# Experts' results weighted at the banks and scattered to the rows of the tokens' choices

## What is computed

```python
def _L1_ffn_ref(hidden_states, gate_w, gate_up_proj, down_proj):
    x = hidden_states.reshape(-1, H)
    probs = jax.nn.softmax(x @ gate_w.T, axis=-1)
    w, idx = jax.lax.top_k(probs, TOP_K)
    w = w / jnp.sum(w, axis=-1, keepdims=True)
    combine = jnp.zeros((T, E), x.dtype).at[jnp.arange(T)[:, None], idx].add(w)
    def step(acc, inputs):
        gup, dn, ce = inputs
        g, u = jnp.split(x @ gup.T, 2, axis=-1)
        acc = acc + ce[:, None] * (jax.nn.silu(g) * u @ dn.T)
        return (acc, None)
    ...
x = x + jnp.tanh(g_ffn[1]) * _L1_ffn_ref(_layernorm(x, axis=-1), ...)
```

## Time and profile before

| | us |
|---|---|
| median of 3 runs (lowest to highest) | 677.53 (677.33 to 678.94) |
| the profiled execution, its own time | 676.72 |
| its span, first to last instruction | 675.0 |
| PE busy in the span | 591.9 (88%) |
| DVE busy | 396.9 (59%) |
| POOL busy | 324.8 (48%) |
| ACT busy | 292.7 (43%) |

### The profile page before, as it was taken

One profiled execution on the slowest core, in us unless ns is written; L12 is line 12 of the kernel. 1 busy time (PEld: TensorE's weight loads), 2 busy tenths in 40 slices (PEclk: granted clock), 3 DMA queues, 4 the chain that ended last, 5 costly groups with the idle time before them and its releaser, 6 DMA issues.

```text
span 675.0 us, 12862 instructions
## 1 busy us (share of the span) xinstructions
PE 591.9 (88%) x5214; PEld 454.9 (67%) x5214; DVE 396.9 (59%) x790; ACT 292.7 (43%) x565; POOL 324.8 (48%) x248
## 2 busy tenths in 40 slices
PE   4699999999889999999999999975299999989920
PEld 3466666667656667676766767554299999889910
DVE  6465557666755455575555656585256666556524
ACT  2144444454433544454444445552066665266300
POOL 4957457755700255453644545594143343234135
PEclk9799999999999999999999999966599999999975
DMA  8900695000000000000000000350421855351024
GB/s 264 303 2 1 252 416 208 2 2 1 3 2 1 1 1 1 1 15 1 15 1 14 15 1 15 147 241 7 163 101 51 349 205 199 121 203 40 26 62 122
DMA packets 22487, 60.33 MB, mean 89 GB/s; under 512 B 3041, under 2 KB 12945, under 8 KB 19089
## 3 DMA queue, kind: packets, MB, share of 16 engines
q1 hardware_dynamic: 19792, 54.82, 21.7%
q0 software_dynamic: 1536, 3.67, 1.8%
q10 hardware_dynamic: 1088, 0.88, 0.5%
HBM read 39.70 MB, written 19.66 MB: 88 GB/s over the span
## 4 chain that ended last, share of the span: by engine, by line
PE 69%; POOL 15%; DVE 8%; issue 3%; ACT 2%; DMA 2%; POOLq 0%; DVEq 0%; ACTq 0%
POOL sr L1442 10%; PE ps L54 8%; PE ps L55 7%; PE ps L56 7%; PE ps L545 6%; PE ps L574 6%; PE ps L622 4%; PE ps L604 4%; PE ps L591 4%; DVE KN L893 3%; PE ps L471 2%; PE ps L654 2%; PE ps L561 2%; PE ps L490 2%; PE ps L430 2%
## 5 line engine op out<-in xcount | busy, mean ns | idle before, releaser
L1473 POOL TENSOR_SCALAR P<-P,rinv 112x487 f32<-112x487 f32 x64 | 97.9, 1540 | 97.6 <-DVE rinv L926 97.6
L1153 POOL TENSOR_TENSOR WL<-WR,WH 128x1024 fp32r<-128x1024 f32 x24 | 60.5, 2519 | 97.2 <-ACT WH L1400 97.2
L1442 POOL TENSOR_TENSOR sr<-sv,mhalf 125x32 f32<-125x32 f32 x16 | 87.0, 5438 | 1.3
L54 PE MATMUL ps<-XGf,WH 128*128 128x256 f32 x256 | 74.0, 289 | 2.1 <-DVE XGf L1088 1.4
L55 PE MATMUL ps<-XGf,WH 128*128 128x256 f32 x256 | 73.6, 288 | 0.0
L56 PE MATMUL ps<-XGf,WL 128*128 128x256 f32 x256 | 73.6, 288 | 0.0
L893 DVE TENSOR_REDUCE KN<-ps 112x4 f32<-112x1500 f32 x32 | 55.0, 1720 | 27.4 <-PE ps L471 27.3
L1279 ACT ACTIVATE P<-ps,nm 112x487 f32<-112x487 f32 x64 | 42.1, 662 | 60.9 <-DVE nm L918 60.9
L1230 ACT ACTIVATE P<-ps 125x1344 f32<-125x1344 f32 x32 | 41.3, 1292 | 43.6 <-PE ps L490 43.6
L918 DVE TENSOR_REDUCE nm<-ps 112x1 f32<-112x487 f32 x64 | 39.5, 659 | 30.4 <-PE ps L591 30.4
L1153 DVE TENSOR_TENSOR WL<-WR,WH 128x1024 fp32r<-128x1024 f32 x24 | 46.9, 1956 | 10.5 <-ACT WH L1400 10.4
(11 more groups left out here) (194 smaller groups left out, 1319.2 us busy)
## 6 DMA issues: line engine op xcount, KB each, us to landing
WR<-in_gupT SPq DMA_DIRECT2D x16, 1024.0 KB, 6.8
WR<-in_dwnT SPq DMA_DIRECT2D x8, 1024.0 KB, 10.5
xs<-ZT SPq DMA_DIRECT2D x14, 512.0 KB, 5.8
ys<-ZT SPq DMA_DIRECT2D x14, 512.0 KB, 6.1
P<-xs SPq DMA_DIRECT2D x24, 128.0 KB, 5.9
CT<-in_ctxT SPq DMA_DIRECT2D x1, 2250.0 KB, 10.4
ys<-WS SPq DMA_DIRECT2D x16, 128.0 KB, 1.8
Wk<-in_L_xattn_Wk SPq DMA_DIRECT2D x2, 512.0 KB, 10.6
```

The costliest lines, as they stand in the source:

```text
L54: e.matmul(out, ah, bh, start=start, stop=False)
L1153: e.tensor_tensor(WL[x % 3][:, cs], WR[x % 3][:, cs], f_(WH[x % 2][:, cs]), ALU.subtract).then_inc(split_done(x, c)[0], 1)
L1442: e.tensor_tensor(sr[:, p, :], sv[:, p, :], mhalf[0:125, 0:32], ALU.pow).then_inc(s("sr"), 1)
L1473: e.tensor_scalar(P[:, k, 0:487], P[:, k, 0:487], rinv[:, k:k + 1], None, ALU.mult).then_inc(s("psc"), 1)
```

## The change

Each row of xs grows from 256 to 258 values (`ROW`): a token's row carries its weight for this choice, tanh of the gate included, and the number of its row in the new ys. For that a second copy of the normalized tokens is kept (`XN2`, copied by ACT, `_2` in the trace), so that the two choices have different tails. ys now has 896 rows for first choices, 896 for second choices, and rows of their own for the empty places of the experts' tiles; it is no longer filled with zeros.

In the experts' loop each load of 128 rows of xs becomes two DMAs, of 256 values into XG and of the last 2 into the tile EX. The copies out of the result banks multiply by the weight in EX. DVE works out the 3 x 128 rows of ys of an expert (`rows_of`, two small operations). SP's stores of results become scatters on POOL, three per expert, the third (`oversent`) also where `over` did not run. At the end SP loads both choices' rows of a sequence with one plain DMA each (8 of 224 KB), and DVE adds the two to X.

```diff
@@ expert_order
             if pdc == 3:
+                put("sent", p)
                 put("over", p)
+                put("oversent", p)
@@ DVE: weights of a token's two choices
-                e.tensor_tensor(q["w1"], q["v1"], q["s2"], ALU.mult).then_inc(s("rchain"), 1)
-                e.tensor_tensor(q["w2"], q["v2"], q["s2"], ALU.mult).then_inc(s("rchain"), 1)
+                for to, v in ((XN, "v1"), (XN2, "v2")):
+                    e.scalar_tensor_tensor(to[:, b, D:D + 1], q[v], q["s2"], tg[0:NQ, 3:4], ALU.mult,
+                                           ALU.mult).then_inc(s("rchain"), 1)
@@ ACT, xtc
+                    if r == 3:
+                        w.wait_ge(s("rconst"), 9)
+                        e.activation(XN2[:, b, 0:D], XN[:, b, 0:D], ACT.Copy).then_inc(s("xn2"), 1)
@@ DVE, hid
-                    n = 4 * i[0] + i[1]
+                    x, n = i[0], 4 * i[0] + i[1]
+                    if i[1] == 1:
+                        for k in (2 * (x % 2), 2 * (x % 2) + 1):
+                            w.wait_ge(s(f"xg{k}"), 32 * (x // 2 + 1))
+                        w.wait_ge(s("xg4"), 32 * (x + 1))
+                        rows_of(e, w, x, slice(0, 3), 2 * x)
...
+        def rows_of(e, w, x, t, at):
+            given = EX[:, x, t, 1].bitcast(I32)
+            w.wait_ge(s("rconst"), 11)
+            e.scalar_tensor_tensor(rows_f[:, x, t], given, 0.0, own[:, x, t], ALU.is_equal,
+                                   ALU.mult).then_inc(s("rows"), 1)
+            w.wait_ge(s("rows"), at + 1)
+            e.tensor_tensor(rows_i[:, x, t], rows_f[:, x, t], given, ALU.add).then_inc(s("rows"), 1)
@@ DVE and ACT, copies out of the banks
-                    e.tensor_copy(YS[:, k, :], ps[:, 5, 0:256]).then_inc(s("yc0"), 1)
+                    e.tensor_scalar(YS[:, k, :], ps[:, 5, 0:256], weight(x, 0), None, ALU.mult).then_inc(s("yc0"), 1)
...
-                    e.activation(YS[:, k, :], ps[:, 6, 0:256], ACT.Copy).then_inc(s("yc1"), 1)
+                    e.activation(YS[:, k, :], ps[:, 6, 0:256], ACT.Copy, scale=weight(x, 1)).then_inc(s("yc1"), 1)
@@ POOL, experts
+                elif stage == "sent":
+                    x, = i
+                    w.wait_ge(s("rows"), 2 * x + 2)
+                    for t_ in range(2):
+                        k = 2 * (x % 2) + t_
+                        w.wait_ge(s(f"yc{t_}"), x + 1)
+                        scatter(e, result_rows(x, t_), YS[:, k, :]).then_inc(s(f"y{k}"), 16)
+                elif stage == "oversent":
+                    x, = i
+                    w.wait_ge(s("tile_act"), 6 * (x + 1))
+                    scatter(e, result_rows(x, 2), YSo).then_inc(s("tile_y"), 16)
@@ POOL, combination
-                    e.indirect_dma_start(Y2[0:NQ, k, :], None, ys,
-                                         bass.IndirectOffsetOnAxis(ap=i_[:, b:b + 1], axis=0)).then_inc(s(f"g{k}"), 16)
@@ SP, experts
-                        e.dma_start(XG[:, k, :], xs[row:row + 128, :]).then_inc(s(f"xg{k}"), 16)
+                        e.dma_start(XG[:, k, :], xs[row:row + 128, 0:D]).then_inc(s(f"xg{k}"), 16)
+                        e.dma_start(EX[:, x, t_, :], xs[row:row + 128, D:ROW]).then_inc(s(f"xg{k}"), 16)
...
-                        e.dma_start(ys[row:row + 128, :], YS[:, k, :]).then_inc(s(f"y{k}"), 16)
@@ SP, combination
+            for k in range(4):
+                w.wait_ge(s(f"y{k}"), 16 * (NE // 2))
+            w.wait_ge(s("tile_y"), 16 * NE)
             for b in range(NB):
-                w.wait_ge(s("comb"), 3 * (b + 1))
+                src = ys[1:1 + 2 * NT, :].rearrange("(c t) d -> t c d", c=2)[b * NQ:(b + 1) * NQ]
+                e.dma_start(Y2[:, b, :, :], src).then_inc(s(f"in_y{b}"), 16)
+            for b in range(NB):
+                w.wait_ge(s("comb"), 2 * (b + 1))
                 e.dma_start(out[b, :, :], X[:, b, :]).then_inc(s("out"), 16)
@@ DVE, combination
+                w.wait_ge(s(f"in_y{b}"), 16)
+                for c in range(2):
+                    w.wait_ge(s("comb"), 2 * b + c)
+                    e.tensor_tensor(X[:, b, :], X[:, b, :], Y2[:, b, c, :], ALU.add).then_inc(s("comb"), 1)
```

More of the change, by code:

```diff
@@ L20 @@
 EPS = 1e-5
+ROW = D + 2
 class Order:
@@ L319, in build, with weight, result_rows, scatter @@
         tri, ones = sq[0:NQ, 0, 0:NQ], sq[0:NQ, 1, 0:NQ]
-        xs = nc.dram_tensor("xs", [NE * NT, D], F).ap()
-        ys = nc.dram_tensor("ys", [NE * NT, D], F).ap()
+        XN2 = B["_2"][0:NQ, 0:NB * ROW].rearrange("p (a b) -> p a b", a=NB)
+        EX = sb("EX", [128, NE, 3, 2])
+        own, own_i, rows_f, rows_i = (sb(n, [128, NE, 3], d) for n, d in
+                                      (("own", F), ("own_i", I32), ("rows_f", F), ("rows_i", I32)))
+        Y2 = B["WR2"][0:NQ, 0:NB * 512].rearrange("p (b c d) -> p b c d", b=NB, c=2)
+        xs = nc.dram_tensor("xs", [NE * NT, ROW], F).ap()
+        ys = nc.dram_tensor("ys", [2 * NT + NE * 3 * 128 + 1, D], F).ap()
+        def weight(x, t_):
+            return EX[:, x, t_, 0:1]
+        def result_rows(x, t_):
+            return bass.IndirectOffsetOnAxis(ap=rows_i[:, x, t_:t_ + 1], axis=0)
+        def scatter(e, rows, src):
+            return e.indirect_dma_start(ys, rows, src, None)
         PTf = PF[:, 1536:5120]
@@ L773, in pairs_out, with sent_before @@
                 w.wait_ge(s(f"pair{k}"), 1 + max(u // 3 for u in before if u % 3 == k))
+        def sent_before(w, x, k):
+            if k:
+                w.wait_ge(s(f"far_y{x}"), 16 * k)
+            else:
+                w.wait_ge(s("tile_y"), 16 * NE)
+                w.wait_ge(s("far_done"), x)
         def skipped(e, sem, before, by):
@@ L1392, in scalar_tile @@
             w.wait_ge(pe, 6 * k + 6)
-            e.activation(YSo, ps[:, 6, 0:256], ACT.Copy).then_inc(act, 1)
+            e.activation(YSo, ps[:, 6, 0:256], ACT.Copy, scale=weight(x, 2)).then_inc(act, 1)
         def split_high(e, w, x, c):
@@ L1467, in pool_attention @@
                                     pattern=[[1, NQ]], channel_multiplier=-1).then_inc(s("rconst"), 1)
+                    w.wait_ge(s("qt2"), NQUAD)
+                    w.wait_ge(s("spk"), order.total["spk"])
+                    w.wait_ge(s("spq"), NB)
+                    for k, to in enumerate((XN, XN2)):
+                        e.iota(to[:, :, D + 1:ROW].bitcast(I32), pattern=[[NQ, NB], [0, 1]], base=1 + k * NT,
+                               channel_multiplier=1).then_inc(s("rconst"), 1)
+                    e.iota(own_i[:, :, :], pattern=[[384, NE], [128, 3]], base=1 + 2 * NT,
+                           channel_multiplier=1).then_inc(s("rconst"), 1)
+                    w.wait_ge(s("rconst"), 10)
+                    e.tensor_copy(own[:, :, :], own_i[:, :, :]).then_inc(s("rconst"), 1)
                 elif stage == "sc":
@@ L1568, in sync_experts @@
                     if x >= 1:
[L1569 removed]
+                        w.wait_ge(s("xg4"), 32 * x)
+                        w.wait_ge(s("tile_pe"), 6 * (x - 1) + 1)
                     row = x * NT + 256
[L1571 to L1588 removed]
+                    e.dma_start(XG[:, 4, :], xs[row:row + 128, 0:D]).then_inc(s("xg4"), 16)
+                    e.dma_start(EX[:, x, 2, :], xs[row:row + 128, D:ROW]).then_inc(s("xg4"), 16)
+                elif stage == "over" and i[0] == 0:
+                    count = counts(e, w)
                 elif stage == "far":
@@ L1640, in _ @@
             pool_experts(e, w)
-            pool_combine(e, w)
         @block.scalar
```

136 lines of the change are left out of this document (57 added, 79 removed).

## The result

The changed kernel took 693.42 us (median of 4 runs, 690.37 to 696.47), beside 677.43 us for the kernel before (4 runs, 676.96 to 678.94): a ratio of 1.0232, 95% interval 1.0183 to 1.0281. The forecast of 668.7 us and its range missed it, on the side of "slower".

The account below looks back on a forecast made before the run. PE bounds the kernel (69% of the chain of waits), except after the last matmul, where it idles 29.80 us. -12.0 + 0.2 + 3.0 = -8.8 us on 676.72 gives 667.9, median 668.7 us; range 664.5 to 677.0.

Parts of the forecast that it names:

- the order on the resource that DVE and POOL share: Among the experts: `hid`, c1, c2, c3 take turns, c3 ends late, PE waits 0.6 us in five experts, +3.0 us.
- the second rival: Among the experts: POOL's c1 gets ahead of DVE's `hid`, 2.1 us for each of five experts; 676.2 us, chance 0.30.
- rows_of: Among the experts: its two small DVE operations cost 0.2 us each and move the following `hid` from 517.40 to 517.80.
- The slack: Among the experts: after PE's wait for c3 the rest follows within PE's slack of some 2 us.
- The scatters: Ahead of c1 in an expert: 1.05 us if awaited, 0.95 us else; 128 rows in proportion add 0.4 us.
- The third rival: Among the experts: scatters slow beside weight loads, deciding from 2.2 us each; at 2.5 us, 682.2 us; chance 0.11.
- Five experts: The wait happens in the first four experts and the sixth, 0.6 us each.
- PE waits for c2: Sign among the experts: PE waiting for c2 would show the prediction wrong.
- Routing to experts: Between routing and experts: DMAs doubled on SP delay PE's third transpose, +0.2 us, bounds 0 to 0.6.
- The end: Last copy to the end: scatters, eight loads and 16 DVE additions finish sooner, -12.0 us, bounds -13 to -10.
- Start and attention: Before routing: dropped zero stores, ACT's copies into XN2 and POOL's new waits together change nothing.

Follow-up runs that it names:

- e1: Changed kernel with rows_of called at an expert's last `hid` instead of the second; 684.22 us, ratio 1.0089.
- e8: Kernel before, with POOL's c1 also waiting for ACT's half for c3, so c1, c3 and c5 run on end; 684.68 us, one run.
- e13: Kernel before, with POOL's c1 waiting for ACT's half for c3 and for DVE's c2 as well; 687.65 us, one run.
- e2: Changed kernel with the three scatters of the first six experts behind POOL's c5 instead of ahead of c1; 669.12 us, ratio 0.9855.
- e12: Changed kernel with DVE's XGf subtraction done twice, so that rows_of comes later by one operation; 691.99 us, ratio 1.0205.
- e5: Changed kernel with only the third scatter of an expert behind POOL's c5, the two others still ahead of c1; 675.83 us, ratio 0.9967.
- e16: Changed kernel with twenty MEMSETs on POOL between the third scatter and c1; 684.95 us, one run.
- e3: Changed kernel with rows_of at the last `hid` and the scatters behind POOL's c5; 667.97 us, ratio 0.9862.
- e6: e3 with DVE's additions at the end done in pairs of tiles; 668.54 us, ratio 0.9861.
- e10: e3 with both results of a token in neighbouring rows of ys; 668.60 us, ratio 0.9856.
- e4: Changed kernel with POOL's c3 waiting for DVE's second `hid`, scatters still ahead of c1; 673.20 us, ratio 0.9923.
- e9: Changed kernel with POOL's c1 waiting for rows_of, scatters still ahead of c1; 672.60 us, ratio 0.9892.
- e7: Changed kernel with the three scatters between POOL's c1 and c3; 677.21 us, ratio 0.9998.
- e14: Changed kernel with one MEMSET on POOL between the third scatter and c1; 687.55 us, one run.

## Why the prediction was wrong

**The step that failed is the order on the resource that DVE and POOL share.** It laid out "`hid` 517.80 to 518.35; c1 from 518.2, as it waits behind it", then c2, then c3: turn and turn about, +0.6 us a period and +3.0 in all. In the changed kernel c1 went ahead of a DVE operation that had come before it, and c3 kept DVE out after c1: +4.5 us a period, +22.8 in all. The moments of arrival were not far off. Counted from the end of the copy, `rows_of` came at 4.31 us (forecast 4.37) and c1 at 4.58 (the forecast had the scatters end at 4.9 and c1 wait for `hid` until 5.2). In the forecast's times that c1 stands at 517.61, ahead of `hid` at 517.80, as in the second rival; but the rival priced this at 2.1 us, because it too let `hid` in at c1's end.

- **rows_of** was priced at 0.2 us an operation from rows of the routing, where POOL had no TENSOR_TENSOR at work. Its first operation has two inputs in SBUF, as `hid` has, and took 5.0 to 5.2 us in five experts, 0.15 us in the others. The kind of DVE's operands alone doesn't decide: the TENSOR_TENSOR at 437.34 in the earlier trace rows has two inputs in SBUF too, and took 0.17 us beside a TENSOR_SCALAR of POOL (first fence below, before). e1 shows that `hid` would have stood there without `rows_of`.
- **The slack.** The sum let c2 in between c1 and c3, as in the kernel before, where POOL's pause of 1.56 us made room for it. But a later c1 uses up that pause: c3 becomes free at a time that ACT sets. With c1 some 2.5 us later within its period, c3 was released before c1 ended, and POOL had no gap left. That the pause would go was to be read off. That DVE would then stand through both operations was not: in e8 and e13 the pause is gone as well, and DVE got in at c1's end.
- **The clock** was not in the sum at all. Of the 4.5 us some 1.7 are PE at 1.2 GHz after the wait.
- **The scatters** were right: 0.97 to 1.00 us alone (forecast 0.95 to 1.05, the proportion for 128 rows did not appear), 1.19 to 1.42 beside c0. The third rival falls: the longest in any run took 1.81 us, not 2.2. The Trainium skill (SBUF — State Buffer, Who interferes with whom) infers that a DVE operation with two inputs in SBUF does not hold up the writing of descriptors. The rows speak against it here too: a scatter took 1.19 us beside c0, and 1.81 us in e2 beside c4; but a scatter also reads its row numbers from SBUF, and no run tells which of the two was held. The Trainium skill (SBUF — State Buffer, SBUF: two separate sides) says of a DVE operation with two SBUF inputs and a POOL operation that reads SBUF that whichever starts first gets the shared ports for the whole instruction, and the other fully blocks. e8's 1.24 us and e13's 1.52 us, let in at c1's end, agree; e12's 4.28 us, where DVE asked before c3 could start, are not explained by it.
- **Five experts**, the first four and the sixth: right. "PE waits for c2" as a sign that the prediction was wrong did not appear in after, only in e5 and e16.
- **Routing to experts** +0.2: no loss shows; from the start of the last scatter of tokens to PE's first transpose it is 5.6 us in both, and PE's wait is 8.4 us, as in the earlier trace rows.
- **The end**: -9.7 instead of -12.0. Three terms were sized too small. The third scatter, started at 674.98, had landed by SP's first load at 678.62, 3.6 us instead of 2.55; the first addition starts 2.9 us after that load's issue instead of 2.3; the additions end at 690.08, 8.56 us instead of 8.0 with waits for loads among them.
- **Start and attention** "nothing": +2.5 us in this profile. POOL and DVE do nearly the same work there; the granted clock from 31 to 43 us is 0.86 before and 0.59 after (second fence below). e3 and e6, with the same start as after, have 0.86 again (third fence: e3) and their first copies at 512.71 and 513.12; e10, which differs from e3 there only in the numbers of the rows, has 0.59 and 515.07. Over all profiles the first copy comes at 512.61 to 514.58 us with the start of before (four profiles) and at 512.71 to 518.12 with that of after (fourteen). So these runs don't show it to be a cost of the change. The +1.8 us of the period with `over` are of the same kind: the waits are the same as before to 0.1 us, the clock fell behind them in after, e1 and e2, and not in e3 and e4. What decides this is not shown.

```profile
434.63 3.01 POOL L1473 TENSOR_SCALAR P<-P,rinv 112x487 f32<-112x487 f32 x2 [1.23 <-DVE rinv L926]
```

```profile
31.00:43.00 12.00, 10.80 (x59) 6.14 (x62) 4.80 (x5) 2.53 (x6) 5.45 (x1) 0.59 0.07 20
```

```profile
31.00:43.00 12.00, 10.44 (x81) 6.14 (x80) 6.32 (x7) 4.46 (x9) 7.66 (x3) 0.86 0.04 12
```

Without the collision the sum nearly holds, but by luck: e3's 668.0 us lies at the forecast's 668.7 because two errors nearly cancel, the 3.0 us among the experts that e3 doesn't lose and the 2.3 us that the end gains less.

## What to carry to other kernels

Where two engines keep each other out, a pause of one can be the other's slot: before work is queued ahead of an operation, look at what idle time it uses up, and whether the operations behind then run on end. Operations that follow each other without a pause need not hold the other engine by themselves (e8); behind scatters they did. A wait put in on purpose (e4, e9) gave back 20 us here and work moved behind the run (e2) 24 us, though no engine had less to do. Price a small operation by its kind of operands and by what works beside it, not by its size, and price a wait of PE with the clock that comes after it.

## What was not expected of the hardware

- A DVE operation of 128x3 values took from 0.15 us to 5.2 us by what POOL did beside it, and c2, 1.23 us alone, up to 8.17 us.
- A scatter at work did not itself hold DVE (0.15 us in e9 and 0.69 us in e7, inside a scatter), but a scatter beside a DVE operation was longer, 1.81 us instead of 0.97 (e2).
- Waits of PE of almost the same length were followed by a lower clock in one place and not in another: 2.54 us in e1 with the clock at 1.00 throughout, 2.83 us in after with 0.50. In e14, with five waits of 3.1 us at most, two of the five periods were 20.8 us and three 22.2 to 22.5.
